# A fused cross-attention kernel: Gram products in 9 instead of 12 matmuls per group, Gram pieces at other places

## The chip, the cores and the metric

The kernel runs on one core of a Trainium2 chip. A core has a matmul engine (TensorE, PE in the profile, with its weight loads listed apart as PEld), VectorE (DVE), ScalarE (ACT), GpSimd (POOL) and SyncE (SP), which here only issues DMAs. The engines run side by side, each works through its own instructions in order, and they wait for each other by semaphores. The metric is the device time of one execution in microseconds, the lower the better.

## The reference, cut to what matters

For each of 8 batches there are 112 query rows `x` (320 channels, 20 heads of 16) and 375 context rows (512 channels), of which the last 4 are "image" tokens.

```
q = x @ W_q;  k = text @ W_k;  v = text @ W_v             # text: 371 context rows
probs = softmax(q k^T / 4)                                # per head, 112 x 371
text_out = probs @ v
qsem = probs @ text;  qsem = qsem / |qsem|                # 512 channels per head and query
sem  = qsem @ (ip / |ip|)^T
probs_ip = softmax(q k_ip^T / 4 + 0.5 * sem) * mask
out = (text_out + probs_ip @ v_ip) @ W_out + b_out + x
```

The norm of `qsem` needs p^T G p for each head and query, where p is the unnormalised softmax row and G = text text^T is the symmetric 371 x 371 Gram matrix of the batch. G and the products with it are what the change is about.

## The kernel before, in words

**Numbers in two parts.** A matrix that needs more precision than the matmul's reduced format is split into a rounded high part and the rest as a low part (`eh`/`el` for the context, `Gh`/`Gl` for G), and the matmuls with both parts are summed.

**Units.** `master_schedule` makes one list of small units of work; every engine walks that list and emits its own share of each unit, so the list is the order of all engines (VectorE alone holds some units back: `behind`). A round is one *group* of 4 heads; there are 5 groups in a batch, 40 in all. The strings `ROUNDS`, `EARLY` (batch 0), `LATE` and `LAST` (batch 7) give the order inside each group. The letters:

- `S0 S1 S2` (unit `St`): transposed scores of the next group, three blocks of 128 tokens by 448 (4 heads by 112). ScalarE turns each into exp (L681, tile `big`) and into a rounded copy `er` (L685).
- `g` or `g2 g1 g0` (unit `gram`): the products of `er` with the block upper triangle of G into one of two PSUM banks `Y`; column block 2 needs three blocks of G, block 1 two, block 0 one, each with `Gh` and `Gl`, so 6 + 4 + 2 = 12 matmuls (L1032). The blocks off the diagonal were doubled when G was stored, since G is symmetric. VectorE multiplies each `Y` with the exps (L829, "product"), GpSimd adds the three results (L547), and `v` (unit `pv`) uses the sum. The third piece, `g0`, writes the bank that the first one used, so it waits for the first product.
- `m` (unit `max`): scores of one head of the next batch; VectorE takes the row maximum (L807). Twenty per batch; `mT` transposes the maxima (L1000) and waits for the last of them.
- `K0 K1 K2`, `G0 G1 G2`, `V0 V1 V2`: pieces of k, G and v of a coming batch. A G piece has 12 matmuls; ScalarE copies the bank to `Gh` (L658, L661), VectorE writes bank minus `Gh` to `Gl` (L799, L801).
- `T0 T1 r0 pw r1 r2 z p pT cT o`: the end of the batch before: transposes of its output, then on VectorE the sum of squares (L867, unit `pw`), on GpSimd a power (L569), three steps to the logits `z` (L593 to L596), on VectorE their maximum (L888, unit `r2`), on ScalarE exp, and so on to the output.

**Ring.** K, G, V, max, mT, T, pT, cT and o write to three PSUM banks `PR` in turn; a unit can start only when the unit three before it in the ring has been read out.

## Time and profile before

| | |
|---|---|
| median of 3 runs | 413.31 us (412.75 to 413.77) |
| the profiled execution | 411.41 us, of which the span from first to last instruction is 409.6 us |
| busy in the span | PE 393.6, PEld 319.5, DVE 220.2, ACT 206.0, POOL 206.3 us |
| granted TensorE clock | 0.997 of full speed |
| chain that ended last | 88% of the span on PE |

The chain of waits is followed back from the last instruction, so its shares say which engine the time hangs on. Matmuls overlap: the duration of one (0.36 us for 448 columns) is longer than the distance from its start to the next one's, and what a matmul costs is that distance. Times in the rows below are microseconds from the start of the span unless marked ns.

### The profile page before, as it was taken

What the parts mean: (1) busy time and instruction counts of PE and PEld (TensorE: products, weight loads), DVE (VectorE), ACT (ScalarE), POOL (GpSimd) and SP (SyncE); (2) the same over time, 40 slices, a digit from 0 to 9 for tenths busy, and PEclk for the clock granted to TensorE, in tenths of its full rate; (3) what the DMA queues carried; (4) which work ended last, traced back from release to release, by engine and by line L of the source; (5) the groups of instructions that cost most, each with busy time, mean ns of one, the idle gap of its engine ahead of it and who ended that gap; (6) DMA issues with size and microseconds to landing.
All of it is one profiled execution on the core that took longest, in us unless ns stands there. A gap on an engine that the chain in (4) does not pass through costs nothing.

```text
span 409.6 us, 9494 instructions
## 1 busy us (share of the span) xinstructions
PE 393.6 (96%) x3653; PEld 319.5 (78%) x3653; DVE 220.2 (54%) x482; ACT 206.0 (50%) x484; POOL 206.3 (50%) x218
## 2 busy tenths in 40 slices
PE   7999799899899999999999999999999999999995
PEld 4648688678788878888789878887888878876762
DVE  0795764575267534665366526663556646643432
ACT  1534134555645565555556564456455366458722
POOL 3020361262527872576437662687247443844981
PEclk9999999999999999999999999999999999999998
DMA  8499994338204802273207511470208210001000
GB/s 259 140 292 234 213 172 84 92 126 166 75 2 150 145 14 72 75 161 61 82 6 193 97 49 36 146 144 18 72 2 168 51 40 2 3 3 39 3 16 15
DMA packets 29455, 38.03 MB, mean 93 GB/s; under 512 B 14361, under 2 KB 26745, under 8 KB 28729
## 3 DMA queue, kind: packets, MB, share of 16 engines
q1 hardware_dynamic: 28514, 36.36, 37.0%
q10 hardware_dynamic: 896, 1.07, 0.9%
q8 instruction: 29, 0.48, 0.5%
q14 instruction: 16, 0.13, 0.1%
HBM read 28.50 MB, written 8.81 MB: 91 GB/s over the span
## 4 chain that ended last, share of the span: by engine, by line
PE 88%; DVE 3%; ACT 2%; issue 2%; DMA 2%; POOL 1%; POOLq 0%; SPq 0%; ACTq 0%; DVEq 0%
PE PR L905 42%; PE Y L905 27%; PE P L905 10%; PE O L905 8%; DMA pb<-wq 1%; DVE big L773 1%; PE PR L1063 1%; ACT big L681 1%; ACT er L685 1%; POOL pb L547 1%; DVE mx L807 1%; DMA qst<-ma 0%; POOLq L169 0%; SPq L460 0%; ACT cTs L729 0%
## 5 line engine op out<-in xcount | busy, mean ns | idle before, releaser
L547 POOL TENSOR_TENSOR pb<-pb 128x448 f32<-128x448 f32 x78 | 89.1, 1142 | 110.4 <-DVE pb L829 104.9
L807 DVE TENSOR_REDUCE mx<-PR 112x1 f32<-112x371 f32 x160 | 83.7, 540 | 78.1 <-PE PR L905 77.1
L905 PE MATMUL Y<-er,Gh 128*128 128x448 f32 x240 | 95.3, 397 | 1.7 <-ACT er L685 0.8
L829 DVE TENSOR_TENSOR pb<-big,Y 128x448 f32<-128x448 f32 x120 | 72.6, 621 | 39.2 <-PE Y L905 39.0
L905 PE MATMUL Y<-er,Gl 128*128 128x448 f32 x240 | 87.3, 364 | 0.0
L681 ACT ACTIVATE big<-P 128x448 f32<-128x448 f32 x120 | 65.2, 543 | 18.7 <-PE P L905 17.9
L685 ACT ACTIVATE er<-big 128x448 fp32r<-128x448 f32 x120 | 69.3, 578 | 3.8
L905 PEld LDWEIGHTS Y<-er,Gh 128*128 128x128 f32 x240 | 45.1, 188 | 13.7 <-DVE pb L829 9.1
L905 PE MATMUL PR<-kst,qst 96*112 96x371 bf16 x160 | 51.3, 331 | 2.2 <-DVE mx L807 2.0
L905 PEld LDWEIGHTS Y<-er,Gl 128*128 128x128 f32 x240 | 45.2, 188 | 2.1
L905 PE MATMUL P<-qst,kst 99*128 99x112 bf16 x480 | 42.0, 214 | 1.5 <-ACT big L681 1.1
L905 PEld LDWEIGHTS P<-qst,kst 99*128 99x128 bf16 x480 | 29.8, 99 | 17.0 <-issue 8.0
L649 ACT ACTIVATE ks<-PR 128x372 bf16<-128x372 f32 (+1 forms) x24 | 10.3, 429 | 47.8 <-PE PR L905 47.2
L905 PE MATMUL PR<-wvh,eh 128*128 128x320 f32 (+1 forms) x96 | 32.3, 336 | 0.2 <-ACT Vt L673 0.2
L673 ACT ACTIVATE Vt<-PR 128x320 f32<-128x320 f32 (+1 forms) x24 | 10.6, 442 | 41.2 <-PE PR L905 41.2
L905 PE MATMUL O<-big,Vt 128*22 128x112 f32 x960 | 31.0, 262 | 0.0
L905 PE MATMUL PR<-eh 128*128 128x376 f32 (+2 forms) x96 | 29.7, 310 | 0.0
L905 PE MATMUL PR<-wvl,eh 128*128 128x320 f32 (+1 forms) x96 | 29.7, 309 | 0.0
L905 PE MATMUL PR<-wvh,el 128*128 128x320 f32 (+1 forms) x96 | 29.6, 309 | 0.0
L569 POOL TENSOR_TENSOR t<-ssq,halfm 112x20 f32<-112x20 f32 (+2 forms) x9 | 28.8, 3202 | 1.4 <-DVE ssq L845 1.3
L905 PE MATMUL PR<-eh,el 128*128 128x376 f32 (+2 forms) x96 | 28.0, 292 | 0.0
L905 PE MATMUL PR<-el,eh 128*128 128x376 f32 (+2 forms) x96 | 28.0, 292 | 0.0
(154 smaller groups left out, 653.5 us busy)
## 6 DMA issues: line engine op xcount, KB each, us to landing
et<-ctxT SPq DMA_DIRECT2D x8, 752.0 KB, 4.4
kst<-kd SPq DMA_DIRECT2D x7, 720.0 KB, 7.2
kd<-ks SPq DMA_DIRECT2D x16, 288.0 KB, 2.9
qst<-qd SPq DMA_DIRECT2D x48, 70.0 KB, 2.4
kst<-kd SPq DMA_DIRECT2D x7, 480.0 KB, 9.9
kst<-kd SPq DMA_DIRECT2D x9, 240.0 KB, 9.0
qd<-kst SPq DMA_DIRECT2D x4, 336.0 KB, 5.6
vx<-xr SPq DMA_DIRECT2D x8, 140.0 KB, 2.2
```

The costliest lines, as they stand in the source:

```text
L547: pool.tensor_tensor(total, total, (pz, pm)[j], ALU.add).then_inc(s_S, 1)
L569: power = pool.tensor_tensor(t1[:, hs], ssq[:, hs], halfm[:, hs], ALU.pow)
L649: act.activation(ks[:, 0, TP * c:TP * c + w], bank[:, 0:w], ACT.Copy).then_inc(s_kh, 1)
L673: act.activation(Vt[b % 2][0:r, i, :, 0:D], bank[0:r, 0:C].rearrange("p (h d) -> p h d", d=D), ACT.Copy).then_inc(s_free[seq[u] % NR], 1)
L681: act.activation(e, P[(3 * g + c) % 2][:, 0:448], ACT.Exp).then_inc(s_exp, 1)
L685: act.activation(er[g % 2][:, 448 * c:448 * c + 448], e, ACT.Copy).then_inc(s_er, 1)
L773: dve.tensor_tensor(kblk[0:w, c, :, :].rearrange("p b (h n) -> p b h n", n=NIP), src, m, ALU.mult).then_inc(s_kb, 1)
L807: dve.tensor_reduce(mx[b % 2][:, h:h + 1], bank[0:S, 0:T], AX.X, ALU.max).then_inc(s_free[seq[u] % NR], 1)
L829: dve.tensor_tensor((pz, pm, pa[g % 2])[j], eb[g % 3][:, 448 * j:448 * j + 448], Y[y % 2][:, 0:448], ALU.mult).then_inc(s_P, 1)
L905: return pe.matmul(o, st, mv, start=start, stop=stop, **kw)
L1063: last = pe.transpose(bank[0:S, 128 * (r - lo):128 * (r - lo) + 128], OT[b % 2][:, r, :], ident[:, :])
```

## The change

A diagonal block of G gets by with one matmul. Its rows are divided by the diagonal (`gc`, the reciprocal `grc`), the exps are multiplied by `gc` when `er` is made, and since only the symmetric part of the block matters, the upper triangle is stored (doubled, with half the diagonal, through the constant masks) and its rounding rest is transposed by TensorE and added into the lower triangle. So a group has 6 matmuls with `Gh` and 3 with `Gl`. For it, VectorE works on each G piece in a chain of six instructions on 128 x 128 or 128 x 1 elements, each waiting for the one before; there is a new unit `D`, a transpose that also takes a place in the ring, with one VectorE instruction behind it; and a new unit `Gl` for the blocks off the diagonal, on VectorE, which in batches 2 to 7 stands behind the second product (`gram` with index 1) of a group. ScalarE's part of G waits for VectorE's fifth instruction and, in those batches, is held until after the next `St` (`late_g`). The strings are rewritten: `g0` stands apart from `g2 g1`, the G pieces stand in the groups 1, 3 and 4 of a batch, `V0` and `V1` earlier, and the masks are loaded where `ident` was one of the later loads.

```diff
-ROUNDS = ("S0 K0 m g m K1 S1 m v S2 m G0 m",
-          "S0 m g m K2 m S1 v m S2 G1 m",
-          "S0 m g2 T0 T1 g1 g0 m r0 G2 m S1 m pw v S2 m V0",
-          "Kr S0 r1 m g m V1 m S1 m m v r2 S2 mT z V2",
-          "p E g pT v cT S0 S1 o S2")
+ROUNDS = ("S0 K0 m m g2 g1 m S1 g0 m m v S2 m K1 m G0",
+          "S0 g2 g1 m S1 g0 m v D0 S2 K2 m V0 m",
+          "S0 g2 g1 m S1 g0 m v T0 T1 r0 S2 V1 m G1 pw m",
+          "Kr S0 r1 g2 g1 m S1 g0 v m D1 m r2 S2 m m mT G2 z V2",
+          "p E g2 g1 pT g0 v D2 cT S0 S1 o S2")
...
-    order += [("G", 0, i) for i in range(3)] + [("K", 1, c) for c in range(3)] + [("Kr", 1)]
-    side = [("V", 0, 0), ("V", 0, 1), ("V", 0, 2)] + [("qip", b) for b in range(B)]
+    order += [u for c in range(3) for u in (("G", 0, c), ("K", 1, c))] + [("Kr", 1)]
+    side = [u for c in range(3) for u in (("V", 0, c), ("D", 0, c))] + [("qip", b) for b in range(B)]
...
@@ VectorE @@
-                    low = dve.tensor_tensor(gl[0:r, o:o + a], bank[0:r, 0:a], gh[0:r, o:o + a].bitcast(f32), ALU.subtract)
...
+                    link(dve.scalar_tensor_tensor(low, bank[0:r, 0:r], 1.0, ident[0:r, 0:r], ALU.mult, ALU.mult, accum_out=c))
+                    link(dve.tensor_scalar(c, c, TINY, None, ALU.max))
+                    link(dve.reciprocal(rc, c))
+                    link(dve.scalar_tensor_tensor(diag, bank[0:r, 0:r], rc, half_upper[0:r, 0:r], ALU.mult, ALU.mult))
+                    dve.scalar_tensor_tensor(low, bank[0:r, 0:r], rc, diag.bitcast(f32), ALU.mult,
+                                             ALU.subtract).then_inc(s_gd if i < 2 else s_free[seq[u] % NR], 1)
...
+                    dve.scalar_tensor_tensor(low, low, c, upper[0:r, 0:r], ALU.mult, ALU.mult).then_inc(s_ru, 1)
+                elif k == "Gl":
+                    dve.wait_ge(s_gh, 3 * b + i + 1)
+                    dve.scalar_tensor_tensor(Gl[b % 2][0:r, LOFF[i]:LOFF[i] + rest], PR[n % NR][0:r, r:r + rest],
+                                             grc[b % 2][0:r, i:i + 1], Gh[b % 2][0:r, o + r:o + r + rest].bitcast(f32),
+                                             ALU.mult, ALU.subtract).then_inc(s_free[n % NR], 1)
+                elif k == "D":
+                    dve.scalar_tensor_tensor(diag, bank[0:r, 0:r], grc[b % 2][0:r, i:i + 1], diag.bitcast(f32), ALU.mult,
+                                             ALU.add).then_inc(s_free[seq[u] % NR], 1)
...
@@ TensorE @@
+                    pe.transpose(bank[0:r, 0:r], dj[i][0:r, 0:r], ident[0:r, 0:r]).then_inc(s_ring, 1)
...
-                        mm(d, Gh[b % 2][:, o:o + 128], mv, i == 0, False)
-                        last = mm(d, Gl[b % 2][:, o:o + 128], mv, False, i == j)
+                        last = mm(d, Gh[b % 2][:, o:o + 128], mv, i == 0, i == j)
+                        if i < j:
+                            o = LOFF[i] + 128 * (j - i - 1)
+                            mm(d, Gl[b % 2][:, o:o + 128], mv, False, False)
```

`EARLY` and `LATE` get `D0 D1 D2` (and `LATE` the split `g2 g1 pT g0`); `LAST` is as it was.

The first place is VectorE in batch 3, from the first product of its group 2 on to the transpose of the maxima. In the kernel before (`Gl` rows: the G pieces; `ssq`: sum of squares; `zm<-z`: maximum of the logits; `ma<-PR`: behind `mT`):

```order
L883 RECIPROCAL rden<-R 112x20
L807 TENSOR_REDUCE mx<-PR 112x1
L799 TENSOR_TENSOR Gl<-PR,Gh 115x115
L807 TENSOR_REDUCE mx<-PR 112x1
L867 SCALAR_TENSOR_TENSOR ssq<-t,R 112x20
L807 TENSOR_REDUCE mx<-PR 112x1 x2
L829 TENSOR_TENSOR pb<-big,Y 128x448 x3
L807 TENSOR_REDUCE mx<-PR 112x1 x4
L888 TENSOR_REDUCE zm<-z 112x20
L814 TENSOR_SCALAR ma<-PR 20x112
```

And there in the changed one, in the piece that the difference rests on:

```order
L841 SCALAR_TENSOR_TENSOR dj<-PR,grc,Gh 128x128
L847 SCALAR_TENSOR_TENSOR dj<-dj,gc,masks 128x128
L925 SCALAR_TENSOR_TENSOR ssq<-t,R 112x20
L865 TENSOR_REDUCE mx<-PR 112x1
L887 TENSOR_TENSOR pb<-big,Y 128x448 x2
L853 SCALAR_TENSOR_TENSOR Gl<-PR,grc,Gh 128x115
L865 TENSOR_REDUCE mx<-PR 112x1
L887 TENSOR_TENSOR pb<-big,Y 128x448
L865 TENSOR_REDUCE mx<-PR 112x1
L860 SCALAR_TENSOR_TENSOR Gh<-PR,grc,Gh 128x128
L865 TENSOR_REDUCE mx<-PR 112x1
L946 TENSOR_REDUCE zm<-z 112x20
L865 TENSOR_REDUCE mx<-PR 112x1 x2
L872 TENSOR_SCALAR ma<-PR 20x112
```

The sum of squares now stands behind the chain of a G piece, and two maxima that stood ahead of the maximum of the logits (`zm<-z`) stand behind it.

The second place is TensorE at the same point, between the sum of squares and `mT`. Before:

```order
L905 MATMUL PR<-wvl,eh 128x320
L905 MATMUL PR<-wvh,el 128x320
L905 MATMUL PR<-kst,qst 112x371
L905 MATMUL P<-qst,kst 128x112 x4
L905 MATMUL PR<-kst,qst 112x371 x2
L905 MATMUL O<-big,Vt 22x112 x12
L905 MATMUL O<-pb,usel 22x112 x4
L905 MATMUL P<-qst,kst 128x112 x4
L1000 MATMUL PR<-ident,mx 20x112
```

In the changed kernel, from the third piece of `gram` on (`PR<-masks,dj` is the new transpose):

```order
L963 MATMUL Y<-er,Gh 128x448
L963 MATMUL O<-big,Vt 22x112 x12
L963 MATMUL O<-pb,usel 22x112 x4
L963 MATMUL PR<-kst,qst 112x371
L1041 MATMUL PR<-masks,dj 128x128
L963 MATMUL PR<-kst,qst 112x371
L963 MATMUL P<-qst,kst 128x112 x4
L963 MATMUL PR<-kst,qst 112x371 x2
L1065 MATMUL PR<-masks,mx 20x112
```

`v` and the last scores no longer stand between the last two maxima and the transpose of the maxima, and the pieces V0 and V1 no longer stand between the sum of squares and it.

## Rows read from the trace of the kernel before

**Rows 1.** Page, costliest groups: the removed kind of matmul, and the row maxima.
```profile
L807 DVE TENSOR_REDUCE mx<-PR 112x1 f32<-112x371 f32 x160 | 83.7, 540 | 78.1 <-PE PR L905 77.1
L905 PE MATMUL Y<-er,Gl 128*128 128x448 f32 x240 | 87.3, 364 | 0.0
```
**Rows 2.** Busy times in one whole batch: PE, PEld, DVE, ACT, POOL, then clock and DMA.
```profile
198.10:242.70 44.60, 44.41 (x442) 37.47 (x439) 23.85 (x54) 24.25 (x57) 25.77 (x25) 1.00 0.37 87
```
**Rows 3.** Timeline (start, duration, what): the end of one group of Gram matmuls.
```profile
227.29 0.62 DVE L829 TENSOR_TENSOR pb<-big,Y 128x448 f32<-128x448 f32 x1 [0.66 <-PE Y L905]
...
227.49 0.36 PE L905 MATMUL Y<-er,Gh 128*128 128x448 f32 x1
227.69 0.37 PE L905 MATMUL Y<-er,Gl 128*128 128x448 f32 x1
...
227.96 0.47 PE L905 MATMUL Y<-er,Gh 128*128 128x448 f32 x1
...
228.27 0.36 PE L905 MATMUL Y<-er,Gl 128*128 128x448 f32 x1
```
**Rows 4.** Waits of the weight loads for the product: us in total, times, longest.
```profile
PEld Y L905 <- DVE pb L829: 9.1, 30, 0.9
```
**Rows 5.** Timeline, from the sum of squares to the transpose of the maxima.
```profile
223.32 0.19 DVE L867 SCALAR_TENSOR_TENSOR ssq<-t,R 112x20 f32<-112x20 f32 x1
...
224.11 3.55 POOL L569 TENSOR_TENSOR t<-ssq,halfm 112x20 f32<-112x20 f32 x1
...
228.55 0.36 POOL L596 TENSOR_TENSOR z<-z,Sip 112x80 f32<-112x80 f32 x1
...
230.39 0.32 PE L905 MATMUL PR<-kst,qst 96*112 96x371 bf16 x1
230.55 0.36 PE L905 MATMUL P<-qst,kst 99*128 99x112 bf16 x4
...
231.37 0.77 PE L905 MATMUL O<-big,Vt 128*22 128x112 f32 x24
...
232.11 0.23 DVE L888 TENSOR_REDUCE zm<-z 112x20 f32<-112x80 f32 x1
232.27 0.37 PE L905 MATMUL P<-qst,kst 99*128 99x112 bf16 x4
...
232.48 0.26 PE L1000 MATMUL PR<-ident,mx 112*20 112x112 f32 x1
```
**Rows 6.** Timeline: two DVE instructions of a chain in which each waits for the last.
```profile
232.78 0.26 DVE L814 TENSOR_SCALAR ma<-PR 20x112 bf16<-20x112 f32 x1 [0.44 <-PE PR L1000]
...
233.07 0.26 DVE L815 SCALAR_TENSOR_TENSOR mr<-PR,ma 20x112 f32<-20x112 f32 x1
```
**Rows 7.** Groups by form on DVE: busy us, mean ns of one, idle before.
```profile
L799 DVE TENSOR_TENSOR Gl<-PR,Gh 128x128 fp32r<-128x128 f32 x16 | 4.6, 287 | 2.4 <-ACT Vt L665 2.4
...
L801 DVE SCALAR_TENSOR_TENSOR Gl<-PR,Gh 128x243 fp32r<-128x243 f32 x8 | 3.2, 401 | 0.0
...
L860 DVE RECIPROCAL zm<-zm 112x8 f32<-112x8 f32 x1 | 0.2, 204 | 0.0
```
**Rows 8.** Timeline: the first K matmul of two batches in turn.
```profile
198.09 0.41 PE L905 MATMUL PR<-eh,wkh 128*128 128x372 f32 x1
...
242.69 0.42 PE L905 MATMUL PR<-eh,wkh 128*128 128x372 f32 x1
```
**Rows 9.** Timeline: the five transposes of unit T.
```profile
218.78 0.71 PE L1063 MATMUL PR<-ident,OT 128*112 128x128 f32 x5
```
**Rows 10.** Timeline, prologue: the transpose of batch 0's maxima, right behind the last maximum.
```profile
63.89 0.26 PE L1000 MATMUL PR<-ident,mx 112*20 112x112 f32 x1 [0.73 <-DVE mx L807]
```
**Rows 11.** Timeline, last batch: the rounded copy that a group's first matmul needs.
```profile
380.29 0.58 ACT L685 ACTIVATE er<-big 128x448 fp32r<-128x448 f32 x1
...
381.01 0.45 PE L905 MATMUL Y<-er,Gh 128*128 128x448 f32 x1
```
**Rows 12.** Timeline, last batch: GpSimd and the sum of squares at once.
```profile
377.42 0.72 POOL L588 TENSOR_TENSOR tn<-R,rden 112x320 f32<-112x320 f32 x1
...
377.48 0.71 DVE L867 SCALAR_TENSOR_TENSOR ssq<-t,R 112x20 f32<-112x20 f32 x1 [1.01 <-POOL t L564]
```

More of the change, by code:

```diff
@@ L132, in behind, with late_g @@
 def behind(order):
+    out, held, low = [], [], []
+    for u in order:
+        if u[0] == "K" and u[1] >= 2:
+            out, held = out + held, [u]
+        elif u[0] == "G" and u[1] < 2 and u[2] < 2:
+            out += [u, ("Gl",) + u[1:]]
+        elif u[0] == "G" and u[2] < 2:
+            out, low = out + low + [u], [("Gl",) + u[1:]]
+        else:
+            out.append(u)
+            if u[0] in ("max", "gram", "mT", "o", "K"):
+                out, held = out + held, []
+            if u[0] == "gram" and u[2] == 1:
+                out, low = out + low, []
+    return out + held
+def late_g(order):
     out, held = [], []
     for u in order:
[L136 to L137 removed]
+        if u[0] == "G" and u[1] >= 2 and u[2] < 2:
+            held.append(u)
         else:
             out.append(u)
[L140 removed]
+            if u[0] == "St":
                 out, held = out + held, []
     return out + held
[L145 removed]
+RING = ("K", "G", "D", "V", "T", "pT", "cT", "o", "max", "mT")
 NR = 3
@@ L225, in build @@
         res = [sb(f"res{i}", [S, C]) for i in range(2)]
+        ident, half_upper, upper = [masks[:, 128 * i:128 * i + 128] for i in range(3)]
         vrT = et[:, 0, 0:H * NIP * 3].rearrange("p (c n) -> p c n", c=3)
@@ L505, in _ @@
             fill(usel[:, :], 0.0)
-            fill(usel[:, 21:22], 1.0)
+            fill(usel[:, 21:22], 2.0)
+            for i in range(2):
+                fill(gc[i][:, :], 1.0)
             fill(half[:, :], 0.5)
@@ L614, in _ @@
             act.dma_start(wv_s, wv.rearrange("(c p) n -> p c n", p=128)).then_inc(s_wr_, 16)
-            for u in order:
+            for u in late_g(order):
                 k = u[0]
@@ L1023, in _ @@
                     if j == 2 and r == 0:
-                        freed(pe, seq[("G", b, 2)])
+                        for i in range(3):
+                            freed(pe, seq[("D", b, i)])
                     if j == 2:
```

78 lines of the change are left out of this document (52 added, 26 removed), and 6 rows, old and new, of the table EARLY.

## The prediction
> **What bounds the kernel now.** I read the busy times by stretch first: in one batch of 44.60 us TensorE is busy 44.41, VectorE 23.85, ScalarE 24.25, GpSimd 25.77, at full clock [rows 2]. TensorE bounds, and the others have some 20 us of room as a mean. A mean does not say where they are waited for, so I then read the timeline of the places that the change touches and the table of waits. A batch takes 242.69 - 198.09 = 44.6 us from one first K matmul to the next [rows 8], so a change in a middle batch counts nearly six times (batches 1 to 6; 0 and 7 have other orders).
>
> **What is removed.** The low matmuls average 364 ns each [rows 1], but the distance between starts is 0.20 us (227.49 to 227.69) [rows 3]; that is what one costs. Three fewer in each of 40 groups: 120 x 0.20 = 24.0 us, 3.0 in a batch. All of it lies on TensorE's path. Second, the wait in a group: the product runs 227.29 to 227.91, `g0` starts at 227.96, and from the last matmul of `g1` to the second of `g0` it takes 0.58 us (227.69 to 228.27) where two distances are 0.40 [rows 3]. So one wait costs 0.18 net (a little more than the shift, since the weights come late too); there are 30 of them, 9.1 us in the weight load's account, which overlaps [rows 4]. With a maximum and a score block between `g1` and `g0` it should go in the middle batches: four groups, 0.75 us a batch. Removed: 3.75 us a batch.
>
> **What is added on TensorE.** Three D transposes a batch. Five transposes in a row take 0.71 us in all, the last one's own 0.27 included, so 0.11 from start to start [rows 9]; with the change of operands I take 0.4 us a batch for three (0.3 to 0.9, the upper end three that overlap nothing).
>
> **What is added on VectorE, and who waits.** A G piece was one or two instructions, the first 287 ns [rows 7]. It is now a chain of six, each released by the one before. In a chain like it the distance is 0.29 us for 0.26 us of work (232.78 to 233.07) [rows 6], so a link costs 0.03. Four instructions over 128 x 128 at 0.29 and two over 128 x 1 at 0.20 (the reciprocal of 112 x 8 takes 0.204 [rows 7]), with links: 4 x 0.32 + 2 x 0.23 = 1.74, say 1.7 us. No row shows a 128 x 1 instruction or one that also writes its sum. From below, six at 0.20 without links make 1.2; from above, six at the 0.40 of the next wider form (128 x 243 [rows 7]) make 2.4. I take 1.7, near the two measured forms.
>
> The Trainium skill has a rule on this, VectorE: DVE Perf Modes, section "The TRN2 errata": every VectorE instruction pays a fixed cost, so many small ones are dear. By its table, 58 cycles for an SBUF source at 0.96 GHz, a 128 x 1 instruction would be 0.06 us and the chain 1.4. The 0.204 of rows 7 speaks for the longer one, and the trace decides.
>
> The load is no problem as a sum (6 us on 23.85 [rows 2]); the place is. Three places:
>
> 1. *Group 4 of a batch, G1.* VectorE's order is G1's chain, sum of squares, and later the maximum of the logits (L888), then the last two maxima; and `mT` on TensorE waits for the last maximum. Between the sum of squares and L888 lies GpSimd: power from 224.11, end of the third `z` step at 228.91, 4.80 us [rows 5]. L888 had 3.2 us to spare (it ran at 232.11). Now the path from G1's last matmul to `mT` is: matmul end to VectorE 0.25, chain 1.7, sum of squares 0.2, hand-over 0.05, GpSimd 4.80, hand-over 0.05, L888 0.23, two maxima 0.46 + 0.54 (540 ns each [rows 1], overlapping by 0.08), hand-over 0.05: 8.3 us. What TensorE has to do meanwhile: six maxima at 0.16 (230.39 to 230.55), two score blocks at 0.21 (232.27 to 232.48), nine Gram matmuls at 0.20, one `v` at 0.90 (231.37 to 232.27) [rows 5], a D at 0.13: 4.2 us, with some 0.3 for changes of kind 4.5. V0 and V1, which used to cover GpSimd's power, now stand ahead of it. So TensorE stands for about 3.8 us in this stretch, mostly in front of `mT`. Within it the wait for the product behind G1's chain is free.
> 2. *Groups 1 and 2.* In group 1 the order m m g2 g1 m g0 m m m K1 gives VectorE, ahead of K1's bank, four maxima and a K rest at 0.5 and three products at 0.6 (0.62 [rows 3]), 4.3 us against TensorE's 4.0; K1 waits 0.3. In group 2 the product waits until G0's chain is done, 0.4. Against that the old order lost 0.3 at such a place: a score block and two maxima take 0.82 us (230.55 to 231.37), where 0.21 + 0.32 would do [rows 5]. Net 0.4 (-0.3 to 1.5).
> 3. *Group 5, G2.* Chain behind `mT`, under V2, twelve matmuls: hidden. The last softmax steps come later by it, 0.1 at pT.
>
> **Sum for one middle batch:** -3.75 + 0.4 + 3.8 + 0.4 + 0.1 = +0.95; times six, +5.7.
>
> **Elsewhere.** Batch 0: `g` in one piece, so a group saves 0.6 but waits 0.2 longer for the product, since `g1` is shorter than it: 5 x -0.4 + 0.4 for D = -1.6. Prologue: the pieces of G of batches 0 and 1 bring six chains, some 7 us more of VectorE, into a stretch where banks come free by VectorE too. Hidden under the K matmuls they cost only the D's 0.4; with half of it exposed 3.5 + 0.4. I take 1.5 (0.4 to 4). The `mT` there waits for the last maximum in any case (0.73 idle [rows 10]); this shows what a maximum right ahead of `mT` costs without any GpSimd. Batch 7: order kept. A group saves 0.6 as long as TensorE bounds; but `er` ends at 380.87 and the group starts at 381.01 [rows 11], so ScalarE's chain is close behind, and group 2 hangs on the sum of squares. I take -1.5 for five groups instead of -3.0 (-2.5 to -0.5). The rest (masks loaded earlier, smaller fills) is under the first DMAs: nothing; uncovered, 0.5.
>
> Sum: 5.7 - 1.6 + 1.5 - 1.5 = +4.1 us on the profiled execution's 411.4, so 415.5. The median of the runs shown is 1.9 above that execution: 413.3 + 4.1 = **417 us**.
>
> **Rivals.**
> *A, the matmuls win (not slower).* If the path through GpSimd is shorter or the order gives it cover that I miss, TensorE still stands for the last two maxima in front of `mT` (about 1.0 us), and 2.8 of the 3.8 us go: 6 x -2.8 = -17 us, so 400. For: 24 us are surely removed from an engine busy 99% of the batch. Against: every term of the 8.3 us is a row, and the order is fixed. Between it and the forecast all is possible: half of the stall gone gives 409. Best case, no new wait at all: 413.3 - 24 - 5 + 3.9 + 1.5 = 390.
> *B, VectorE backs up further (slower still).* Chains of 2.3 us and 1.5 us of lag in groups 1 and 2: 6 x (0.7 + 0.7) = +8.4, so 425. For: the ring has three banks, and every D and G piece takes one. Against: 20 us of room.
> *C, GpSimd holds up the new chain.* The sum of squares, which reads two tiles of SBUF, took 0.71 us and ended with GpSimd's instruction, where it otherwise takes 0.19 [rows 12, 5]. The chain's last instruction also reads two (`dj`, the mask). GpSimd has nothing to do at G1's place, but at G0's and G2's it may: if the 0.5 us of that row is lost there and falls on the path, 6 x 2 x 0.5 = +6, so 423; on G0's alone 420. The rule stands in the Trainium skill, SBUF — State Buffer, "Who interferes with whom": a VectorE instruction with two SBUF inputs waits while a GpSimd one that reads SBUF holds the shared interface. The trace agrees.
> *D, the removed matmuls don't count,* because weight loads set the pace. PEld is busy 37.47 of 44.6 [rows 2], and a load goes with each matmul; they leave together. Hardly any chance.
>
> **Chances.** Forecast (414 to 420) 0.42; A and what lies between, 0.34; B 0.12; C 0.10; D 0.02. Less than 0.3% (1.2 us) can't be told from no change here. Faster 0.32, same 0.12, slower 0.56. The range 401 to 422 leaves out the far ends of A and of B. For the forecast alone it is 413 to 421.
>
> **What would show it.** In the profile after: 120 fewer low matmuls, still 0.20 apart; six VectorE instructions per G piece in 1.7 us; TensorE idle 1.5 to 2.5 us in front of `mT` in each of batches 1 to 6, put down to the maximum, with L888 waiting for GpSimd's `z` just before; a middle batch of 45.5 us; the first Gram group 1.5 us later. If a middle batch takes under 43.5 us, or L888 does not wait for `z`, the forecast is wrong; if the chain is under 1.4 us or over 2.1, its size is.

## The result, and the profile after

The changed kernel takes 442.46 us (median of 4 runs, 440.77 to 445.99) against 413.53 (412.75 to 413.77) of the kernel before: ratio 1.0713, 95% interval 1.0667 to 1.0759. Forecast were 417, with a range to 422. The direction was right and the size was not: 29 us where I had 4. The medians in this document are over all executions of a run; the ratios leave out those more than 1.5% above the fastest of their kernel.

The page of the changed kernel, in the form of [rows 1]: the low matmuls, the maxima, the scaled copy, and the clock in 40 slices.
```profile
PEclk9999889899999979998999989998999899999998
...
L865 DVE TENSOR_REDUCE mx<-PR 112x1 f32<-112x371 f32 x160 | 83.2, 538 | 54.4 <-PE PR L963 53.3
...
L719 ACT ACTIVATE er<-big,gc 128x448 fp32r<-128x448 f32 x120 | 80.4, 670 | 3.9
...
L963 PE MATMUL Y<-er,Gl 128*128 128x448 f32 x120 | 44.3, 369 | 0.0
```
The same line of the kernel before:
```profile
PEclk9999999999999999999999999999999999999998
```
The 120 matmuls are gone. New is the clock line: in the profile of before, no stretch ahead of the tail was below full speed; now there are dips at regular distances. Over the span the mean granted clock is 0.962 (0.997 before).

One middle batch of the changed kernel, answering [rows 2] (same columns).
```profile
217.98:266.06 48.08, 44.34 (x428) 37.14 (x426) 28.21 (x74) 25.82 (x55) 25.69 (x25) 0.96 0.33 79
```
48.1 us, not 44.6; TensorE has 3.7 us of holes, and VectorE 4.4 us more to do (I had 6).

VectorE's chain for the G1 piece of that batch (start, duration, what).
```profile
243.02 0.29 DVE L837 SCALAR_TENSOR_TENSOR dj<-PR,masks 128x128 f32<-128x128 f32 x1 [0.92 <-PE PR L963]
243.24 0.08 DVE L837 DVE_READ_ACCUMULATOR dj<-PR,masks 128x1 f32 x1
243.36 0.15 DVE L838 TENSOR_SCALAR gc<-gc 128x1 f32<-128x1 f32 x1
243.54 0.16 DVE L839 RECIPROCAL grc<-gc 128x1 f32<-128x1 f32 x1
243.74 0.35 DVE L840 SCALAR_TENSOR_TENSOR Gh<-PR,grc,masks 128x128 fp32r<-128x128 f32 x1
244.13 0.35 DVE L841 SCALAR_TENSOR_TENSOR dj<-PR,grc,Gh 128x128 f32<-128x128 f32 x1
244.51 0.35 DVE L847 SCALAR_TENSOR_TENSOR dj<-dj,gc,masks 128x128 f32<-128x128 f32 x1
244.78 0.19 DVE L925 SCALAR_TENSOR_TENSOR ssq<-t,R 112x20 f32<-112x20 f32 x1
```
The chain runs 243.02 to 244.86, 1.84 us, and the sum of squares right behind it. Then GpSimd, and VectorE's end of the path, answering [rows 5].
```profile
245.05 3.55 POOL L602 TENSOR_TENSOR t<-ssq,halfm 112x20 f32<-112x20 f32 x1 [3.21 <-DVE ssq L925]
...
249.48 0.35 POOL L629 TENSOR_TENSOR z<-z,Sip 112x80 f32<-112x80 f32 x1
```
```profile
249.87 0.24 DVE L946 TENSOR_REDUCE zm<-z 112x20 f32<-112x80 f32 x1 [0.90 <-POOL z L629]
250.02 0.98 DVE L865 TENSOR_REDUCE mx<-PR 112x1 f32<-112x371 f32 x2
```
TensorE in the same place: its last maxima, the transpose `mT` that waits, and V2 behind it.
```profile
248.31 0.62 PE L963 MATMUL PR<-kst,qst 96*112 96x371 bf16 x2 [0.17 <-DVE mx L865]
251.15 0.26 PE L1065 MATMUL PR<-masks,mx 112*20 112x112 f32 x1 [2.22 <-DVE mx L865]
...
253.09 0.47 PE L963 MATMUL PR<-wvh,el 128*115 128x320 f32 x1
253.36 0.47 PE L963 MATMUL PR<-wvh,eh 128*115 128x320 f32 x1
```
TensorE stands for 2.22 us, as forecast (1.5 to 2.5). Ahead of it, in the same stretch from G1's last matmul on, it also stood for 0.71 us in front of the held-back `g0` (at 246.01) and for 0.17 in front of the last two maxima: 3.1 us together, where I had 3.8. What I had not foreseen is behind it: the matmuls of V2 start 0.27 us apart (253.09 and 253.36), where those of V1 in the kernel before start 0.15 apart:
```profile
229.07 0.30 PE L905 MATMUL PR<-wvh,eh 128*128 128x320 f32 x1
229.22 0.31 PE L905 MATMUL PR<-wvl,eh 128*128 128x320 f32 x1
```
The windows of busy time (columns as in [rows 2]) show why.
```profile
248.50:251.10 2.60, 0.43 (x2) 0.13 (x1) 1.60 (x5) 0.89 (x2) 2.22 (x6) 1.00 0.64 107
251.10:252.40 1.30, 1.25 (x13) 1.28 (x14) 0.85 (x4) 0.00 (x0) 1.30 (x2) 0.98 0.00 0
252.40:255.80 3.40, 3.40 (x15) 3.40 (x15) 2.25 (x10) 0.40 (x2) 0.37 (x2) 0.51 0.02 4
```
From 252.4 to 255.8 the granted clock is 0.51: the lower level, 1.2 GHz, 1.2 us after the idle ended. Five of the six middle `mT` have such a stretch behind them, 3.4 us long (6.8 in batch 1), beginning 0.3 to 1.5 us after the idle; and the prologue has two, 6.8 and 3.4 us.

The waits of TensorE over the whole span, and VectorE's for `z` (us in total, times, longest; L946 is the L888 of before).
```profile
PE PR L1065 <- DVE mx L865: 14.1, 7, 2.2
PE Y L963 <- DVE pb L887: 8.4, 18, 1.0
PE PR L963 <- DVE mx L865: 4.9, 9, 3.3
```
```profile
DVE zm L946 <- POOL z L629: 7.2, 7, 1.7
```

By stretch, from the first Gram matmul of each batch in both traces: the prologue (to 75.34 before, 84.52 after) costs 9.2 us more; batch 0 0.4 less; batches 1 to 6 together 22.0 more (259.7 and 281.7); batch 7 with the tail 1.4 less.

**Time at full clock.** Executions of one kernel differ mostly in their clock: the four of the changed kernel have spans of 439.0, 440.9, 440.4 and 444.2 us at mean granted clocks of 0.962, 0.956, 0.956 and 0.949. Span times clock is 422.3, 421.5, 421.0 and 421.5. Where TensorE is the bound, half clock loses half of the stretch, so this figure is an estimate of what the span would be without it. For the kernel before it is 408.9 (407.4 to 411.3 in the runs beside the experiments). So of the 29 us about 13 are work and waits, and 16 are clock. The figure stands beside each median in the table; it is worked out, not measured, and exact only as far as TensorE bounds the slow stretches. Where the long stalls were filled with extra matmuls, so that the clock mostly stayed up (e2, e8 below), it is 423.8 and 424.8, 2 to 3 us higher: read the clock's share as 13 to 16 us.

### The profile page after: what moved, and what is told of

Its sections match the earlier page's. It is cut to its first block, busy times and chain, and to the rows that moved or that the text cites. A ratio compares the mean times of both kernels' runs of the same rounds, so it can differ in the third digit from the quotient of the medians.

```text
span 439.0 us, 9501 instructions
## 1 busy us (share of the span) xinstructions
PE 395.3 (90%) x3557; PEld 316.6 (72%) x3557; DVE 257.2 (59%) x650; ACT 217.5 (50%) x460; POOL 205.3 (47%) x220
## 4 chain that ended last, share of the span: by engine, by line
PE 56%; DVE 16%; POOL 12%; issue 6%; DMA 4%; ACT 3%; SPq 1%; POOLq 0%; DVEq 0%; ACTq 0%
PE PR L963 35%; PE Y L963 10%; POOL t L602 6%; PE O L963 5%; DMA et<-ctxT 4%; PE P L963 3%; DVE pb L887 3%; POOL pb L580 2%; DVE mx L865 2%; DVE Gh L840 1%; DVE dj L841 1%; DVE dj L837 1%; DVE kr L815 1%; PE PR L1041 1%; DVE big L808 1%
## 5 line engine op out<-in xcount | busy, mean ns | idle before, releaser
L963 PE MATMUL Y<-er,Gh 128*128 128x448 f32 x240 | 89.6, 399 | 10.0 <-DVE pb L887 8.4
L719 ACT ACTIVATE er<-big,gc 128x448 fp32r<-128x448 f32 x120 | 80.4, 670 | 3.9
L963 PEld LDWEIGHTS Y<-er,Gh 128*128 128x128 f32 x240 | 46.1, 192 | 20.7 <-DVE pb L887 16.0
L963 PE MATMUL PR<-kst,qst 96*112 96x371 bf16 x160 | 49.8, 336 | 5.0 <-DVE mx L865 4.7
L963 PE MATMUL Y<-er,Gl 128*128 128x448 f32 x120 | 44.3, 369 | 0.0
L963 PEld LDWEIGHTS P<-qst,kst 99*128 99x128 bf16 x480 | 31.4, 99 | 16.5 <-issue 6.6
L963 PE MATMUL PR<-wvh,eh 128*128 128x320 f32 (+1 forms) x96 | 35.7, 372 | 0.4 <-DVE mx L865 0.2
L963 PE MATMUL PR<-wvl,eh 128*128 128x320 f32 (+1 forms) x96 | 33.2, 346 | 0.0
L963 PE MATMUL PR<-wvh,el 128*128 128x320 f32 (+1 forms) x96 | 33.0, 343 | 0.0
L963 PE MATMUL PR<-eh 128*128 128x376 f32 (+2 forms) x96 | 30.6, 319 | 0.1
L963 PEld LDWEIGHTS PR<-kst,qst 96*112 96x112 bf16 x160 | 20.4, 130 | 13.4 <-DVE mx L865 6.1
L963 PEld LDWEIGHTS O<-big,Vt 128*22 128x22 f32 x960 | 21.0, 101 | 9.5 <-issue 8.8
```

The lines of the kernel that those rows point to most:

```text
L719: act.activation(er[g % 2][:, 448 * c:448 * c + 448], e, ACT.Copy, scale=gc[g // NG % 2][:, c:c + 1]).then_inc(s_er, 1)
L963: return pe.matmul(o, st, mv, start=start, stop=stop, **kw)
```

## The experiments

| run | edit | median us | ratio to before, 95% | at full clock |
|---|---|---|---|---|
| before | | 412.2 to 413.5 | 1 | 408.9 |
| changed | | 442.46 | 1.071 (1.067 to 1.076) | 421.5 |
| e1 | power ahead of G1 | 432.14 | 1.043 (1.036 to 1.049) | 416.8 |
| e2 | busy in front of `mT` | 432.63 | 1.050 (1.043 to 1.057) | 423.8 |
| e3 | before, nine matmuls | 402.35 | 0.975 (0.971 to 0.979) | 394.3 |
| e4 | prologue's old order | 444.34 | 1.076 (1.072 to 1.080) | 423.0 |
| e5 | before, nine, held back | 394.43 | 0.955 (0.950 to 0.959) | 389.1 |
| e6 | changed, old rounds | 438.20 | 1.062 (1.058 to 1.067) | 427.5 |
| e7 | e1, maxima earlier | 434.55 | 1.050 (1.043 to 1.056) | 414.7 |
| e8 | busy, prologue too | 431.32 | 1.046 (1.040 to 1.052) | 424.8 |
| e9 | before, held back | 412.33 | 1.000 (0.997 to 1.002) | 408.3 |
| e10 | plain copy to `er` | 442.56 | 1.072 (1.069 to 1.076) | 420.9 |
| e11 | chain of three | 432.70 | 1.044 (1.039 to 1.050) | 413.0 |
| e12 | before, late maxima | 418.24 | 1.015 (1.010 to 1.019) | 414.3 |
| e13 | prologue chains short | 441.38 | 1.066 (1.059 to 1.074) | 419.1 |
| e14 | as e12, power later | 417.61 | 1.012 (1.007 to 1.017) | 414.9 |
| e15 | chains under V | 438.74 | 1.062 (1.056 to 1.068) | 426.4 |
| e16 | as e12, 1.75 us idle | 429.46 | 1.035 (1.026 to 1.044) | 417.9 |
| e17 | e5, load behind bank | 418.79 | 1.016 (1.010 to 1.023) | 409.8 |
| e18 | e5, load ahead of it | 438.69 | 1.051 (1.040 to 1.060) | 422.8 |

**The clock in front of `mT` (e2, e12, e14, e16).** First the gap is filled.
```diff
+                    if b >= 2:
+                        for _ in range(16):
+                            mm(bank[:, 0:256], wvh[:, 0, 0:128], wkh[:, 0, :], True, True)
                     freed(pe, seq[("max", b, H - 1)])
```


> The changed kernel with 16 extra matmuls of 256 columns on constants, written into mT's own bank right before mT waits for the last maximum, in batches 2 to 7 (their result is overwritten by mT). The wait stays as it is; only TensorE is not idle in it. Theory (the clock falls because TensorE idled 2.2 us there): the granted clock stays at its upper level at all middle mT places, V2 takes 1.8 us again in place of 3.3, and the time falls by 5 x 1.5 = 7 to 10 us, to 432 to 436. Rival (the clock falls for another reason, or the half-speed stretch costs nothing since something else is waited for): 441 to 444 or, if the extra matmuls run on past the maximum, up to 2 us more.

The window of the batch, columns as in [rows 2]:
```profile
213.46:260.00 46.54, 44.73 (x443) 37.44 (x442) 28.36 (x74) 25.95 (x55) 25.70 (x25) 1.00 0.35 84
```
Clock 1.00, 46.5 us in place of 48.1; batches 1 to 6 take 272.4 in place of 281.7. `mT` starts 8.4 us after G1's last matmul, nearly as before (8.5), so nearly all of these 9.3 us are the clock; half of the 20.5 us that the changed kernel spends there at the lower level would be 10.2. Theory right.

Then the idle is put into the old kernel, complete with its twelve matmuls.
```diff
-          "S0 m g2 T0 T1 g1 g0 m r0 G2 m S1 m pw v S2 m V0",
-          "Kr S0 r1 m g m V1 m S1 m m v r2 S2 mT z V2",
+          "S0 m g2 T0 T1 g1 g0 m r0 G2 m S1 m v S2 m V0",
+          "Kr S0 m pw r1 g m V1 m S1 v r2 S2 m m mT z V2",
```


> The kernel before, complete, with GpSimd's power behind V0 and a maximum (some 3.4 us later) and the last two maxima right in front of mT, so that TensorE, busy for the rest of each batch with all twelve matmuls a group, stands in front of mT for 1.2 to 1.8 us in batches 1 to 6. Theory (an idle of that size in front of mT is enough for the clock to fall, whatever else was changed): half-speed stretches behind at least two of the six mT, 420 to 432. Rival (the clock falls because TensorE has less to do in the whole batch): no such stretch, the idles alone, 419 to 423.

It was 1.02 us of idle at each of six places, a batch 1.0 us longer, and the clock stayed up (0.995). The size of the idle was guessed too high, so this told only that 1.0 is harmless in such a batch. For a longer one, first `r1 g pw` in place of `pw r1 g`, roughly:
```diff
+          "Kr S0 m r1 g2 pw g1 g0 m V1 m S1 v r2 S2 m m mT z V2",
```


> The kernel before, complete, with the last two maxima right in front of mT as in the run with the late maxima, and GpSimd's power another step later, between the first and second block of group 5's Gram (sum of squares 1.4 us later): TensorE stands 1.8 to 2.8 us in front of mT in batches 1 to 6, and has all twelve matmuls a group besides. Theory (an idle of that length is enough for the fall, whatever the rest of the batch): the clock falls to its lower level behind most of the six mT, 6 x 0.9 to 1.5 for the longer idle and 4 to 9 for the clock over the 418.2 of the shorter idle: 427 to 437. Rival (it takes a batch with less work in it as well): no half-speed stretch there, 423 to 428.

A miss: with `r1` ahead of the power its steps no longer wait for it (they read an older power here, which is what this kernel changes in the computation), the path through GpSimd is short again, and the idle stayed at 1.02. It tests nothing. With `pw r1` kept together:
```diff
+          "Kr S0 m g2 pw r1 g1 g0 m V1 m S1 v r2 S2 m m mT z V2",
```


> The kernel before, complete, with the last two maxima right in front of mT and GpSimd's power, followed by r1, between the first and second block of group 5's Gram: the sum of squares is 1.4 us later than in the run with the late maxima (idle 1.02 there), so the idle in front of mT should be 1.8 to 2.4. Theory (an idle of that length is enough, in a batch otherwise as busy as before): half-speed stretches behind most of the six mT and a mean clock under 0.985: 427 to 435. Rival (it takes less work in the batch as well): clock 0.99 and more, 422 to 428.

Timeline and windows of that run, batch 3:
```profile
241.26 0.34 PE L1000 MATMUL PR<-ident,mx 112*20 112x112 f32 x1 [1.76 <-DVE mx L807]
```
```profile
239.00:241.30 2.30, 0.54 (x8) 0.23 (x5) 1.14 (x3) 1.34 (x4) 2.00 (x5) 0.98 0.00 0
241.30:244.80 3.50, 3.50 (x14) 3.50 (x15) 1.52 (x6) 0.27 (x1) 1.94 (x4) 0.53 0.01 1
```
With 1.75 us of idle the clock falls behind five of six `mT`, in a kernel that lacks none of its matmuls: 11 us over e12, of which 3.6 are at full clock and the rest the clock. The fall comes at once here, within 0.1 us of `mT`. The theory holds, the rival falls. The Trainium skill, TensorE: Matmul & The Clock Gate, section "HAM oscillation — how this bites in real kernels", tells of a loop in which TensorE waits for a DMA in each turn, 3 to 5 us, and starts the next turn at the lower clock. This trace agrees in kind, in five of six batches; its waits are shorter, 1.75 us.

**The path to `mT` (e1, e7).** GpSimd's power one step forward:
```diff
-          "S0 g2 g1 m S1 g0 m v T0 T1 r0 S2 V1 m G1 pw m",
+          "S0 g2 g1 m S1 g0 m v T0 T1 r0 S2 V1 m pw G1 m",
```


> The changed kernel with GpSimd's power (and with it the sum of squares on VectorE) ahead of the G1 piece in group 4 of batches 1 to 6. Theory (path plus clock: GpSimd's start hangs on G1's chain, the stall in front of mT follows, and the clock falls behind the stall): the path to mT is shorter by G1's 12 matmuls (1.5), its chain (1.85) and the hand-over (0.25), 3.6 us, so that L946 no longer waits for z in the middle batches, TensorE idles under 1 us in front of mT, and the granted clock stays at its upper level there: 48.1 us a middle batch becomes 44 to 45.5, and the whole 418 to 427. Rival 1 (only the wait, no clock effect): 2.2 us idle goes in each of six batches, 429. Rival 2 (the rest is VectorE's and ScalarE's added load, the place of G1 does not matter): 439 to 443.

The idle in front of `mT` is 1.22 us in all six batches, and L946 no longer waits for `z` in them: the wait through GpSimd was real, worth 4.7 us at full clock. But the clock still fell behind five of the six in the profiled execution (clock 0.963; the other three had 0.971 to 0.978), and 432 us is above the theory's range and rival 1's 429: the wait went, the clock did not come back. Then the maxima as well:
```diff
-          "Kr S0 r1 g2 g1 m S1 g0 v m D1 m r2 S2 m m mT G2 z V2",
+          "Kr S0 r1 g2 g1 m S1 g0 m D1 m m m v r2 S2 mT G2 z V2",
```


> The changed kernel with GpSimd's power ahead of the G1 piece, and in group 5 the three maxima right behind D1, with v, r2 and the score block between the last of them and mT. Theory: with power ahead alone 1.22 us of idle stayed in front of mT, that of the last two maxima, and the clock fell behind five of six of them; v (0.9) and the score block (0.2) now cover it: idle under 0.5 us in front of mT, no half-speed stretch in the middle batches, a middle batch 44 to 45, the whole 417 to 424. Rival (the clock falls for the activity of the whole batch, not for this idle): stretches at the lower level stay, 426 to 431.

No idle is left in front of `mT`, and in the profiled execution (429.94 us, clock 0.971) only two of six middle batches have a slow stretch; in the other three executions the clock was 0.952 to 0.956, as low as in the changed kernel. The longest idles left in the middle batches are of 0.6 us, and both slow stretches begin within 0.9 us of the end of one. A middle batch at full clock takes 45.6, more than expected. So `mT` was not all: neither for the clock nor for the work.

**What was removed (e3, e5, e9).** In the old kernel:
```diff
-                        mm(d, Gh[b % 2][:, o:o + 128], mv, i == 0, False)
-                        last = mm(d, Gl[b % 2][:, o:o + 128], mv, False, i == j)
+                        last = mm(d, Gh[b % 2][:, o:o + 128], mv, i == 0, i == j)
+                        if i < j:
+                            mm(d, Gl[b % 2][:, o:o + 128], mv, False, False)
```


> The kernel before with nothing changed but the Gram groups: the low matmul of the three diagonal blocks is left out, nine matmuls in place of twelve (this leaves out the low part of G's diagonal blocks). Order, G pieces, VectorE, ScalarE and GpSimd as before. It prices the 120 matmuls alone. My term: 120 x 0.20 = 24 us less, less what then waits for the product: 392 to 397 if TensorE stays the bound in all groups. Rival (without the third matmul ahead of the product's release the group waits for VectorE's product, since g1 is then only three matmuls, and the other engines' chains come closer): half of it, 400 to 406.

Less than my term: a middle batch 42.8, 1.8 shorter and not 3.0. TensorE now waits 4.2 us for the product in the whole kernel, where it was 0.6. Then `g` becomes `g2 g1 m S1 g0` in each round:

> The kernel before with nine matmuls per group (the low part of G's diagonal blocks is left out) and the last block of each group behind a maximum and a score block (g2 g1 m S1 g0), G pieces and everything else where they were. With the block not held back nine matmuls gave 402.4, 1.8 us less in a middle batch where my term said 3.0. Theory: the missing 1.2 is TensorE waiting for the product, since two of the three blocks are now a low matmul shorter; held back, it comes back together with my 0.75: 6 x 1.2 to 6 x 1.95 less, 391 to 396. Rival (the product's wait only moves: banks of the maxima and score blocks are late instead): 400 to 404.

A middle batch 41.85, and 394.43 us: 20 us at full clock below the kernel before, as expected here. It is the fastest of all, but it leaves out the low part of the diagonal blocks. Its batch, for comparison with the changed one:
```profile
197.16:239.01 41.85, 41.44 (x425) 35.00 (x423) 23.41 (x53) 24.74 (x58) 25.71 (x25) 1.00 0.40 93
```
And the same order with all twelve matmuls:

> The kernel before, complete, with its twelve matmuls per group and one thing changed: the last block of each group stands behind a maximum and a score block (g2 g1 m S1 g0). My term for this was 0.75 a batch, 4.5 in six: 407 to 410. Theory (with twelve matmuls the product is waited for by 0.18 per block only, so holding back gives about that; the 8 us it gave with nine came from the 1.2 a batch that nine left open): 407 to 411. Rival (the gain belongs to the new places of S1 and the maxima and is as large as with nine): 403 to 406.

No change in the time (408.3 against 408.9 at full clock); a middle batch is 44.44 us. So holding back is worth 0.16 us a batch with twelve matmuls, and 0.97 with nine. What rows 3 have as a wait does not go: behind a score block, the first matmul of the held block is still 0.29 us ahead of its neighbour, where 0.20 is usual.
```profile
232.45 0.45 PE L905 MATMUL Y<-er,Gh 128*128 128x448 f32 x1
232.74 0.37 PE L905 MATMUL Y<-er,Gl 128*128 128x448 f32 x1
```
The two savings depend on each other: 1.8 and 0.16 us a batch alone, 2.7 together, where I had 3.75. e9 was the version that might have beaten the kernel before with the whole computation; it does not.

**What was added (e6, e10, e11, e15).** The changed computation with the rounds of the kernel before (G0, G1, G2 at their old places, D0 to D2 behind them, and the last part of a G piece behind the next maximum or Gram block):

> The changed kernel's computation (nine matmuls, chains of six, D transposes, scaled copies, its prologue) with the rounds of the kernel before: groups in one piece, G0, G1, G2 in groups 1, 2, 3, V1 and the score block between the last maximum and mT; D0, D1, D2 behind them in groups 2, 3, 4. Theory (what is lost in the middle is the order: G1's chain ahead of GpSimd's path and the last two maxima right in front of mT): TensorE idles under 0.5 us in front of mT, the clock stays at its upper level in the middle batches, a middle batch takes 43 to 44.5 in place of 48.1: 415 to 424 in all, and only the prologue's 9 us stay. Rival (the chains cost VectorE too much wherever they are, and TensorE waits for banks): 46 us and more a batch, 430 or more.

The rival: 47.3 us a batch at full clock (0.8 more than the new order has with its gap filled, 46.5 in e2). In front of `mT` nothing over 0.6 us is left, but TensorE now stands 1.7 us in front of a held product and 1.2 in front of T. With ScalarE's plain copy:
```diff
-                    act.activation(er[...], e, ACT.Copy, scale=gc[g // NG % 2][:, c:c + 1])
+                    act.activation(er[...], e, ACT.Copy)
```


> The changed kernel with the copy into er as it was, without its scale by gc (this leaves out the scaling of the exponentials): 578 ns in place of 670 for each of 120 copies, 11 us less on ScalarE in all. Theory (ScalarE is not waited for in the middle of the kernel): 440 to 443; in groups where a score block waits for a bank of P, up to 0.3. Rival (ScalarE's lateness is part of the 1.9 us that TensorE loses at score blocks in a middle batch): 433 to 438.

Nothing: ScalarE's 11 us are hidden. With three of the chain's six instructions:
```diff
-                    link(dve.tensor_scalar(c, c, TINY, None, ALU.max))
-                    link(dve.reciprocal(rc, c))
...
-                    dve.scalar_tensor_tensor(low, low, c, upper[0:r, 0:r], ALU.mult, ALU.mult).then_inc(s_ru, 1)
+                    dve.sem_inc(s_ru, 1)
```


> The changed kernel with three of the six instructions of each G piece's chain left out: the floor, the reciprocal and the last product with the mask (this leaves out the scaling of G and the mask on its low part). The chain is 0.75 us shorter: 1.1 in place of 1.85. Theory (the chain's length stands on the path to mT once, and in front of the held-back g0 in groups 1, 2 and 4): mT's idle 1.4 to 1.6 in place of 2.2, and 1.0 to 2.0 us less in a middle batch before anything on the clock; 430 to 436, and lower where the shorter idle leaves the clock up. Rival (the place of the chain and its waits count, not its length; the instructions left out hide in other waits): 439 to 443.

10 us less, 8.5 of them at full clock, so the length counts; but the idle in front of `mT` is 2.22 as before, since TensorE comes to `mT` earlier too: the 0.71 us in front of `g0` behind G1's chain are 0.18. What shrank is TensorE's wait for the product, from 8.4 us to 2.9:
```profile
PE Y L962 <- DVE pb L886: 2.9, 12, 1.0
```
And each chain under a V piece (the rounds of groups 1 to 4; the late parts of a G piece no longer held):
```diff
+ROUNDS = ("S0 K0 m m g2 g1 m S1 g0 m m v S2 m K1 m",
+          "S0 g2 g1 m S1 g0 m G0 V0 m v S2 K2 m",
+          "S0 g2 g1 m S1 g0 m T0 T1 r0 D0 pw G1 V1 m v S2 m",
+          "Kr S0 r1 g2 g1 m S1 g0 m m D1 m m v r2 S2 mT G2 z V2",
```


> The changed kernel's computation, complete, in another order: each G piece right ahead of a V piece (G0 V0 in group 2, G1 V1 in group 3, mT G2 z V2), so that its chain on VectorE runs under V's 1.8 us of matmuls; GpSimd's power ahead of G1; three maxima no longer right in front of mT but v and a score block between; ScalarE's and VectorE's later parts of a G piece no longer held back. Theory (place, not load): the waits for the product go, a middle batch takes 42.5 to 44.0 at full clock, no idle over 1 us in it and no half-speed stretch: 408 to 418. Rival (load: the chains, D and the third bank are late wherever they stand): a middle batch of 45 and more, 424 or more.

The rival again, 426.4 at full clock. TensorE's longest account is now a bank of the ring that VectorE frees late:
```profile
PE PR L963 <- DVE Gl L853: 8.9, 6, 1.7
```

**Late, or holding a bank (e17, e18).** Into e5, five linked products of 128 x 128 for each G piece of batches 2 to 7, behind the release of its bank or ahead of it.
```diff
+                    for n in range(5 if b >= 2 else 0):
+                        link(dve.tensor_tensor(dj[0:r, 0:r], ident[0:r, 0:r], ident[0:r, 0:r], ALU.mult))
```


> The old kernel with nine matmuls a group, the last block held back (the low part of G's diagonal blocks is left out), and on VectorE five linked products of 128 x 128 more for each G piece of batches 2 to 7, behind the instruction that frees its bank: 5 x 0.32 = 1.6 us, 4.8 in a batch, as load alone. Without them it was 394.4 (span times clock 389). Theory (lateness: products, maxima and the sum of squares queue behind a chain, and TensorE waits in its group): 0.5 to 1.0 us per piece, 9 to 18 in six batches: 402 to 412. Rival (the bank is what counts): 394 to 398.

> The same with the five instructions ahead of the one that frees the bank, so that the G piece's bank, one of three, is also held 1.6 us longer. Theory (lateness alone counts): as with the load behind, within 2 us of it. Rival (the bank counts, alone or on top): 4 to 15 us more than with the load behind.

At full clock 389.1 becomes 409.8 with the load behind, 20.7 us for 18 loads: over a microsecond each, more than the theory allowed. The load was longer than planned, though. Seven of the 18 took 1.6 us, and GpSimd was idle during these. The other eleven took 2.3 or more beside instructions of GpSimd: one of the five products, which have two SBUF inputs, then took up to 1.0 us instead of 0.29. The mean is 2.0. One of the eleven, with what GpSimd ran beside it:
```profile
221.38 2.28 DVE L806 TENSOR_TENSOR dj<-ident 128x128 f32<-128x128 f32 x5
221.34 0.87 POOL L561 TENSOR_TENSOR vx<-vx,hv 80x320 f32<-80x320 f32 x1
```
Ahead of the release the load takes 2.1 us in the mean, about the same, and the time becomes 422.8. Both causes are real, and the second adds 13. TensorE's waits in one batch, first e17, then e18 (window 197 to 245):
```profile
PE Y L908 <- DVE pb L832: 1.5, 1, 1.5
PE PR L908 <- DVE mx L810: 1.3, 1, 1.3
```
```profile
PE PR L908 <- DVE Gl L802: 2.2, 1, 2.2
PE PR L1067 <- DVE Gl L804: 2.1, 1, 2.1
PE PR L908 <- DVE Gl L804: 0.8, 1, 0.8
```
The Trainium skill, Perfetto Trace Analysis, section "Matmuls", advises to rotate matmul groups through different banks, so that the emptying of one overlaps the next one's matmuls. The kernel does that with three; e18 against e17 shows what it costs when one of them is emptied up to 2 us later.

**The prologue (e4, e8, e13).** The old order of its pieces (three G, then three K):
```diff
-    order += [u for c in range(3) for u in (("G", 0, c), ("K", 1, c))] + [("Kr", 1)]
+    order += [("G", 0, i) for i in range(3)] + [("K", 1, c) for c in range(3)] + [("Kr", 1)]
```


> The changed kernel with the prologue's order as it was: the three G pieces of batch 0 in a row, then the K pieces of batch 1. Theory (the prologue's 9.2 us come from K1.0 standing right behind G0.0 and waiting for el, from the chains in VectorE's queue ahead of the copies that free banks, and from half-clock stretches behind the idles): with G0 first the wait for el (1.75 us) goes, and the first Gram group starts 2 to 5 us earlier: 437 to 441. Rival 1 (the three chains in a row then hold D, and the ring's banks, longer): 442 to 446, slower. Rival 2 (the idle behind it is what counts, and it stays): within 1 us of 442.5.

Not faster (rival 1, 1.5 us more at full clock). The first Gram group starts at 82.69, 1.8 us earlier, but with one slow stretch of 3.4 us ahead of it in place of the two: the new order is not the fault. Extra matmuls in the stalls, beside those of e2:
```diff
+                for _ in range({("max", 0, 2): 28, ("K", 2, 0): 9}.get(u, 0)):
+                    mm(Y[1][:, 0:256], wvh[:, 0, 0:128], wkh[:, 0, :], True, True)
```


> The changed kernel with extra matmuls of 256 columns on constants in every long stall: 16 in front of mT in batches 2 to 7, and in the prologue 28 in front of the third maximum (idle 3.35 us there) and 9 in front of batch 2's first K piece (idle 1.17). All waits stay. Theory: with those of mT alone it was 432.6; the half-speed stretches of the prologue (6.8 and 3.4 us) go too, and give back 3 to 6 us there: 426 to 430, clock above 0.99. Rival (in the prologue TensorE is not what ends last, so its clock costs nothing): 431 to 434.

The first Gram group starts 2.6 us earlier than in the changed kernel and batch 0 takes 2.6 longer (35.2 to 37.8), since a stretch at the lower clock falls there, and an idle that a DMA ends: the rival. (This execution also had a slow stretch of 3.4 us at 30.6, ahead of all stalls filled here.)
```profile
113.58 0.55 PE L963 MATMUL P<-qst,kst 99*128 99x112 bf16 x8 [1.61 <-DMA qst<-ma]
```
And the chains of batches 0 and 1 cut to two instructions each:

> The changed kernel with four of six instructions of the chains of batches 0 and 1 left out, all in the prologue (this leaves out the scaling of those two batches' G and the mask on its low part); batches 2 to 7 as they were. Six chains become 1.1 us shorter, 6.6 us of VectorE. Theory (the prologue is paced by VectorE: chains stand ahead of the copies and maxima that free banks): the first Gram group starts 3 to 6 us earlier than 84.5, and the whole takes 436 to 440. Rival 1 (the start of batch 1 hangs on the data of K through memory, so what the prologue gains is given back in batch 0, as with the extra matmuls in the prologue, where 2.6 came and 2.6 went): first group 3 to 5 us earlier, the whole within 1.5 of 442.5. Rival 2 (the D transposes and order pace it): first group under 1 us earlier.

The first group starts at 80.86, 3.7 us earlier, and the whole is not measurably faster (441.4). At full clock it is 2.4 better; the profiled execution has a mean clock of 0.952, and the one of the four with 0.964 took 436.9. Not all of the 3.7 us are the chains': 1.1 were there before the first of them ran (VectorE's copy into `el` right ahead of it starts at 34.42 here and at 35.49 in the changed kernel; in the other runs anywhere from 34.1 to 38.2), and about 1.4 come from the second slow stretch, which here falls behind the first group. The four instructions left out of each chain are worth some 1.2 us of the prologue's 9. Where TensorE stood in the changed kernel, and what VectorE did then:
```profile
52.45 0.56 PE L963 MATMUL PR<-kst,qst 96*112 96x371 bf16 x1 [3.35 <-DVE mx L865]
```
```profile
47.37 0.69 DVE L803 TENSOR_TENSOR sq<-ET_IP 128x128 f32<-128x128 f32 x1
47.99 3.96 DVE L808 TENSOR_TENSOR big<-kipT,hq 128x640 f32<-128x640 f32 x3
```
In the kernel before the same place had 1.84 us of idle. With the short chains (e13) it still had 3.49, so they are not what it waits for; and 50.9 to 57.7 is now at half clock.

## Why the prediction was wrong

*The stall in front of `mT`: right.* Place, order and size: 2.22 us of idle, L946 waiting for `z` just before it, the chain 1.84 us (I had 1.7; its two 128 x 1 instructions took 0.15 and 0.16 us, between the 0.06 and the 0.20 that the prediction names, and three of the four wide ones 0.35 where I had 0.29). e1 confirms the path.

*Full clock throughout: wrong, and the largest error.* The prediction starts from "at full clock" and puts the clock at nothing after the change too, without a reason. No sentence of mine gave the stall a second price, though in [rows 2] TensorE stood for only 0.2 us of a whole batch. e2 prices it at 9.3 us in the middle batches, and e16 shows that an idle of 1.75 us brings it about. With the prologue's stretches it is 13 to 16 of the 29.

*"Removed: 3.75 us a batch": measured 2.7 (e5), 41.85 in place of 44.57.* The 3.0 of the matmuls is right only if nothing waits for the product behind the shorter blocks (1.8 alone, e3); the 0.75 for holding back is 0.16 by itself (e9). The mistake is in how I read [rows 3 and 4]: most of the 0.18 was not a wait for the product, since the first matmul of the block costs nearly as much behind a score block; and the low matmuls that go had covered a wait that opens without them. Even with the block held back, the matmuls that go are worth 2.6 us (44.44 to 41.85) and not 3.0, and that 0.4 is not put down to anything. Six batches: 6 us.

*What is added: right in sum, which is partly luck.* My terms were 0.4 + 3.8 + 0.4 + 0.1 = 4.7; at full clock e2's batch stands 46.54 - 41.85 = 4.7 above e5's. But the stretch to `mT` has 3.1 of it and not 3.8, 2.2 of them in front of `mT`. The other held-back blocks wait some 0.5 us a batch for the product behind a chain (1.2 in e2's batch, of which 0.7 belong to the stretch to `mT`), near my 0.4 for groups 1 and 2. That leaves some 0.7 us that no run puts down to anything, and it is by chance that they make up for what the first term had too much. With the term for what is removed and one for the clock right, my own sum for a middle batch would have been 45.5 + 1.0 + 1.6 of clock, which is the 48.1 measured.

*Batch 0 -1.6: it was -0.4. Batch 7 -1.5: it was -1.4.*

*Prologue +1.5: it was +9.2, outside my 0.4 to 4.* The stretches at lower clock (6.8 us, and 2.9 of the second) count for up to half their length, 5; four of the six instructions of each chain for about 1.2 (e13), which is near my own term; about 3 us are not put down to anything. I had not looked for the place where a 4-us job of VectorE (L808) stands in front of the maxima.

*The whole.* The profiled executions differ by 29.4 us where I had 4.1. Of the 25 us between, 9.3 are the clock in the middle batches, 6 what was removed, 8 the prologue (up to 5 of them clock) and 1 batch 0.

*Rivals.* A (the matmuls win) is what the old kernel does without the chains (e5), not this one. B (VectorE backs up further) is the nearest: waits of 0.7 to 1.0 in front of held blocks, though the chain took 1.84 us and not 2.3. C (GpSimd holds up the chain) did not come: none of the 24 instructions of L847 took over 0.354 us. But GpSimd ran nothing beside any of them, so C's condition never arose; the loads of e17, beside which it did run, show the delay. D is out by e3, which is 2.5% faster. None of them had the clock.

*Still open.* What decides whether the clock falls. In the changed order it fell with 1.22 us in front of `mT` in five of six batches (e1), and with no idle over 0.65 us in two of six (e7); in the old one it never fell with 1.02 (e12, e14) and fell with 1.75 in five of six (e16); but in e18 idles of 2.10 and 2.25 us stood in nearly every middle batch and the clock stayed at full level for 191 us of the profiled execution. Length alone does not tell it. Open too are some 3 of the prologue's 9.2 us.

## What to carry to other kernels

Price a new stall of TensorE twice: its length, and the slower matmuls that may stand behind it; multiply span and mean granted clock to keep the two apart when runs scatter. Two savings at the same wait do not add up from their separate readings; a run with each alone and one with both cost little. In this kernel 2 us more work on an engine that is 56% busy (23.41 of 41.85) cost 1.15 us of the bound where it stood behind the release of a buffer of the small ring, and 1.9 us ahead of it.

## What I had not expected of the hardware

- Behind most idles of 1.2 to 2.2 us in front of `mT`, in a kernel that is otherwise busy, the granted clock went to its lower level for 3.4 or 6.8 us. It fell 0.3 to 1.5 us after work had begun again in the changed kernel, 0.8 to 1.8 in e1 and at once in e16. The matmuls of V then start 0.27 us apart instead of 0.15.
- One kernel had mean clocks of 0.952 to 0.971 (e7) or 0.949 to 0.962 (the changed one) in executions of the same run; the time moved by 9 and 5 us with it.
- Instructions on VectorE whose result is one column of 128 took 0.15 and 0.16 us; one that also sums its output brings a second of 0.08 us; a product with a scalar per partition took 0.35 us where the two-operand one took 0.29 [rows 7]. ScalarE's copy with a scale per partition took 670 ns, without it 578 ns.
- A VectorE product with two SBUF inputs took up to 1.0 us instead of 0.29 while a GpSimd instruction ran (e17), at 11 of 18 places; at the other seven, with GpSimd idle, none was slow.
